# Sorted experts: rings of eight blocks, destinations read in place, the second bias staged with the weights, experts chosen by maxima, part 0 placed ahead of later projections

## The reference

```python
x = _layernorm(x + L1_attn(x, ...))
logits = flat_x @ W_router + b_router              # 2048 tokens, 8 experts
top_vals, top_idx = jax.lax.top_k(logits, 2)
w = softmax over the two chosen logits
for e in range(8):
    h = relu(flat_x @ W1[e] + b1[e])               # 128 -> 512
    y = h @ W2[e] + b2[e]                          # 512 -> 128
    final_output += y * w[:, e]                    # 0 for tokens that did not choose e
x = _layernorm(x + final_output)
```

## Time and profile before

| | us |
|---|---|
| median of 3 runs | 2021.28 (2018.37 to 2021.78) |
| profiled execution, its own time | 2016.37 |
| its span, first to last instruction | 2014.6 |

### The profile page before, as it was taken

The page is one execution under the profiler, slowest core; times in us unless marked ns, Lnnn a source line. Parts: engine busy times, 40 slices in busy tenths (PEclk is TensorE's granted clock), DMA queues, the critical chain, the costliest instruction groups (busy, mean ns, idle before and its releaser), DMA issues. The chain is left out here.

```text
span 2014.6 us, 42506 instructions
## 1 busy us (share of the span) xinstructions
PE 1725.4 (86%) x15741; PEld 1463.1 (73%) x15741; DVE 1403.6 (70%) x3312; ACT 999.9 (50%) x2616; POOL 605.6 (30%) x1005
## 2 busy tenths in 40 slices
PE   3599999899999999999993797999999999986583
PEld 2577778788778778787872564788888888876473
DVE  4688777787777887777873675666666666645456
ACT  2355555555555555555551324566565656533242
POOL 6255335554345553345450000000000000013431
PEclk9799999999999999999996798999999999996797
DMA  4122332123332323322331104940000000020112
GB/s 187 53 70 62 72 82 73 43 70 74 72 82 52 64 62 71 83 65 57 76 62 41 45 0 63 116 2 1 1 2 2 1 2 1 1 85 24 51 54 82
DMA packets 145232, 106.20 MB, mean 53 GB/s; under 512 B 32068, under 2 KB 134296, under 8 KB 144008
## 3 DMA queue, kind: packets, MB, share of 16 engines
q1 hardware_dynamic: 142760, 98.85, 23.3%
q0 software_dynamic: 2272, 4.67, 0.7%
HBM read 86.39 MB, written 17.10 MB: 51 GB/s over the span
## 5 line engine op out<-in xcount | busy, mean ns | idle before, releaser
L577 POOL TENSOR_TENSOR kfull<-kt,pair_rows 128x512 f32<-128x512 f32 x128 | 143.9, 1124 | 514.2 <-ACT kt L365 504.2
L345 PE MATMUL ps<-xT,taps 128*128 128x128 f32 x2176 | 295.0, 278 | 0.1
L345 PEld LDWEIGHTS ps<-xT,taps 128*128 128x128 f32 x2176 | 275.6, 197 | 8.0 <-issue 7.6
L830 ACT COPY wt<-ps 32x128 f32<-32x128 f32 x512 | 131.7, 257 | 259.4 <-PE ps L726 253.1
L1562 DVE TENSOR_REDUCE b_nmax<-ps 128x1 f32<-128x128 f32 (+7 forms) x256 | 180.4, 752 | 73.0 <-PE ps L1397 73.0
L873 DVE TENSOR_TENSOR prod<-ps,mt 128x128 f32<-128x128 f32 x512 | 147.1, 287 | 74.6 <-PE ps L737 59.3
L726 PE MATMUL ps<-ident,w 128*128 128x128 f32 x512 | 162.3, 317 | 34.2 <-ACT wt L830 19.8
L1539 POOL COPY b_spread<-b_inv 128x256 f32<-128x256 f32 x64 | 25.8, 403 | 512.9 <-DVE b_inv L1565 512.9
L876 DVE TENSOR_REDUCE w<-prod 128x32 f32<-128x128 f32 x512 | 146.5, 286 | 17.5
L726 PEld LDWEIGHTS ps<-ident,w 128*128 128x128 f32 x512 | 87.8, 171 | 84.8 <-DVE w L876 73.4
L1489 ACT ACTIVATE b_prob_long<-ps,b_nmax 128x1024 f32<-128x1024 f32 (+3 forms) x128 | 121.4, 953 | 55.7 <-DVE b_nmax L1562 55.7
(11 more groups left out here) (294 smaller groups left out, 3881.5 us busy)
## 6 DMA issues: line engine op xcount, KB each, us to landing
decay<-ends_dram SPq DMA_DIRECT2D x256, 128.0 KB, 5.8
gn<-near_dram SPq DMA_DIRECT2D x34, 384.0 KB, 6.8
rr<-rates_dram SPq DMA_DIRECT2D x34, 256.0 KB, 4.6
sq<-rstd_dram SPq DMA_DIRECT2D x17, 512.0 KB, 3.7
slots_dram<-zero SPq DMA_DIRECT2D x1, 8704.0 KB, 60.8
wtap<-in_taps SPq DMA_DIRECT2D x4, 1024.0 KB, 11.3
f_w<-in_f_w SPq DMA_DIRECT2D x2, 2048.0 KB
s_xb<-slots_dram SPq DMA_DIRECT2D x39, 64.5 KB, 1.8
```

The lines of the kernel that those rows point to most:

```text
L345: mm = pe.matmul(part, lhsT=taps[:, tap, t * P:(t + 1) * P], rhs=xT[:, :, columns(at_next) - LOOK + tap:columns(at_next) - LOOK + tap + TS ...
L577: nc.gpsimd.tensor_tensor(kfull[:, n % 4, :, :], kt[:, n % 2, :].unsqueeze(1).to_broadcast([P, G, P]), cst["pair_rows"][:, :].unsqueeze(2) ...
L830: nc.scalar.copy(wt[rows, b, :], ps[rows, 2, 0:P]).then_inc(wt_kept[b], 1)
```

## The change

- The rings of x rows and results have eight buffers (`AHEAD`). The wait for the scatter of block k-8 stands in `keep_y` and in SP's load, no longer in `stage`; `stage` waits for `y_kept` of block k-3 instead.
- Destinations are stored as integers in the rows' last column, and the scatter reads them there; the cast and `y_i` are gone. The fill of empty slots writes integers too.
- b1 and b2 lie beside w2 (`DOWN` = 644 columns for each expert), and one copy stages all. `keep_y` adds b2. The bias matmuls, the transposes of the weights and the four adds are gone.
- `choose` takes the maximum twice (`pick`) and works on 32 columns. The difference of the two scores is kept, one Exp over all tiles runs on ACT at block 2, and `share_out` at block 8 turns it into shares.
- `positions` adds the counts of earlier tiles up in PSUM by 8 matmuls instead of 2; `place_rows` is shorter.
- Order: part 0 is normalized, chosen and placed ahead of part 1's norm; projections of parts 1 and 3 are cut in halves, with `turn_x(0)`, `logit(0)` and `positions(1)` in between. ACT does part 2's squares ahead of `keep_x(1)`, and part 3's ahead of `keep_x(2)`.
- `HALVES` is 1, so all branches for more than one half are not taken; lines that serve them alone are left out here, as are declarations and the bodies that only vanish (`bias`, `weigh`, `exponent`, `keep_comb`, the old `choose` and the loops that called them), which stand in the kernel above.

```diff
-    nc.gpsimd.memset(blank[2][:, :], 0.0).then_inc(fill_made, 1)
-    pool.wait_ge(fill_made, 2)
-    nc.gpsimd.tensor_copy(blank[1][:, :], blank[0][:, :]).then_inc(fill_made, 1)
+    nc.gpsimd.memset(blank[1][:, :], 0.0).then_inc(fill_made, 1)
...
-SLOTS = NT * P
...
+SLOTS = NT * P // HALVES
+BLOCKS = TOP * NT // HALVES + NE - 1
+STRETCH = NE * SLOTS + NE * P
...
-        if k >= 4:
-            sp.wait_ge(S["x_turned"], k - 3)
-            sp.wait_ge(S["staged"], k - 3)
...
+    for k in range(K):
...
+        if k >= AHEAD:
+            sp.wait_ge(y_out[k % AHEAD], 16 * (k // AHEAD))
+        at = sp.value_load(table_i[0:1, 0, k:k + 1], min_val=0, max_val=HALVES * STRETCH - P)
+        sp.dma_start(xb[:, k % AHEAD, :], x_dram[bass.ds(at, P), :]).then_inc(xb_in[k % AHEAD], 16)
...
+    def send_result(k):
+        pool.wait_ge(S["y_kept"], k + 1)
+        nc.gpsimd.indirect_dma_start(
+            out=y_dram[:, :], out_offset=bass.IndirectOffsetOnAxis(
+                ap=xb[:, k % AHEAD, C:ROW].bitcast(U32), axis=0),
+            in_=yb[:, k % AHEAD, :], in_offset=None).then_inc(y_out[k % AHEAD], 16)
...
+    for t in range(GT):
+        ch.step(nc.gpsimd.tensor_copy(row[:, t, :, :, C:ROW].bitcast(I32), place[:, t, :, :, :]))
...
-        pe.wait_ge(S["made"], 1)
-        chosen = of(sel, s).rearrange("p t e -> p (t e)")
-        pe.matmul(small(s)[:, 32:64], lhsT=before[:, :], rhs=chosen, start=True, stop=True, skip_group_check=True)
-        pe.matmul(small(s)[:, 64:96], lhsT=ones[:, :], rhs=chosen, start=True, stop=True,
-                  skip_group_check=True).then_inc(S["pos_done"], 1)
...
+        if s == 0:
+            pe.wait_ge(S["made"], 1)
+        mine = of(sel, s).rearrange("p t e -> p (t e)")
+        pe.matmul(small(s)[:, 32:64], lhsT=before[:, :], rhs=mine, start=True, stop=False, skip_group_check=True)
+        for t in range(1, GT):
+            pe.matmul(small(s)[:, 32 + t * NE:64], lhsT=ones[:, :], rhs=mine[:, 0:(GT - t) * NE], start=False,
+                      stop=(t == GT - 1), skip_group_check=True)
         for t in range(GT):
...
+            mm = pe.matmul(small(s)[:, 64:64 + NE], lhsT=ones[:, :], rhs=mine[:, t * NE:(t + 1) * NE], start=(t == 0),
+                           stop=(t == GT - 1), skip_group_check=True)
+        mm.then_inc(S["pos_done"], 1)
...
-        if k < 2:
-            pe.wait_ge(S["bias_added"], 1)
-        else:
+        if k == 0:
+            pe.wait_ge(S["slotted"], PARTS - 1)
+            pe.wait_ge(S["in_done"], PARTS)
+        if k >= 2:
             pe.wait_ge(S["rect_a"], k - 1)
             pe.wait_ge(S["rect_v"], k - 1)
...
-        if k < 2:
-            pe.wait_ge(S["bias_added"], 1)
-        else:
+        if k >= 2:
             pe.wait_ge(S["y_kept"], k - 1)
+        if k == 1:
+            pe.wait_ge(S["slotted"], PARTS)
...
     project(0)
-    project(1)
+    project(1, range(0, 2))
     turn_x(0)
     logit(0)
+    project(1, range(2, GT))
+    positions(0)
     project(2)
-    positions(0)
     turn_x(1)
     logit(1)
-    project(3)
-    bias(0)
+    project(3, range(0, 2))
+    positions(1)
+    project(3, range(2, GT))
     turn_x(2)
     logit(2)
-    positions(1)
-    bias(1)
+    positions(2)
     turn_x(3)
     logit(3)
-    positions(2)
-    bias(2)
-    positions(3)
-    bias(3)
+    if HALVES == 1:
+        positions(3)
...
+    squares(0)
+    root(0)
+    keep_x(0)
+    squares(1)
+    root(1)
+    squares(2)
+    keep_x(1)
+    root(2)
+    squares(3)
+    keep_x(2)
+    root(3)
+    keep_x(3)
+    keep_block(0)
...
+        rectify(k)
+        if k == 2:
+            act.wait_ge(S["gaps"], PARTS)
+            nc.scalar.activation(share[:, 1, :], best[:, :, 1], ACT.Exp).then_inc(S["exp_done"], 1)
...
+    def pick(s, w):
+        level = of(best, s)[:, :, w]
+        mine = chosen[:, s, w, :, :]
+        ch.step(reduce(level, score[:, :, :], axis=AX.X, op=ALU.max))
+        ch.step(tt(hit[:, :, :], score[:, :, :], level.unsqueeze(2).to_broadcast(square), ALU.is_equal))
+        ch.step(tt(hit[:, :, :], hit[:, :, :], order[:, :].unsqueeze(1).to_broadcast(square), ALU.mult))
+        ch.step(reduce(where[:, :], hit[:, :, :], axis=AX.X, op=ALU.max))
+        ch.step(tt(mine, hit[:, :, :], where[:, :].unsqueeze(2).to_broadcast(square), ALU.is_equal))
     def choose(s):
         dve.wait_ge(S["logits"], s + 1)
...
         if s == 0:
             dve.wait_ge(S["made"], 1)
...
+        ch.step(tt(score[:, :, :], small(s)[:, 0:32].rearrange("p (t e) -> p t e", t=GT),
+                   br[:, :].unsqueeze(1).to_broadcast(square), ALU.add))
+        pick(s, 0)
+        ch.step(nc.vector.scalar_tensor_tensor(out=score[:, :, :], in0=chosen[:, s, 0, :, :], scalar=LOWEST,
+                                               in1=score[:, :, :], op0=ALU.mult, op1=ALU.add))
+        pick(s, 1)
+        tt(of(sel, s), chosen[:, s, 0, :, :], chosen[:, s, 1, :, :], ALU.add).then_inc(S["sel_done"], 1)
+        tt(of(best, s)[:, :, 1], of(best, s)[:, :, 1], of(best, s)[:, :, 0], ALU.subtract).then_inc(S["gaps"], 1)
+    def place_rows(s):
+        g, i = divmod(s, PG)
+        dve.wait_ge(S["pos_done"], s + 1)
+        ch.step(tt(slot[:, :, :], small(s)[:, 32:64].rearrange("p (t e) -> p t e", t=GT),
+                   seen[:, g, i, :].unsqueeze(1).to_broadcast(square), ALU.add))
+        ch.step(tt(seen[:, g, i + 1, :], small(s)[:, 64:64 + NE], seen[:, g, i, :], ALU.add))
+        by = [P, TOP, GT, NE]
+        ch.step(tt(picked[:, :, :, :], chosen[:, s, :, :, :], slot[:, :, :].unsqueeze(1).to_broadcast(by), ALU.mult))
+        ch.step(reduce(pair[:, :, :], picked[:, :, :, :], axis=AX.X, op=ALU.add))
+        ts(slot_i[:, s, :, :], pair[:, :, :], float(g * STRETCH), None, ALU.add).then_inc(S["slotted"], 1)
...
         if k >= 2:
-            dve.wait_ge(S["down_done"], k - 2)
             dve.wait_ge(S["up_done"], k - 1)
         if k >= 3:
+            dve.wait_ge(S["y_kept"], k - 2)
             dve.wait_ge(S["rect_a"], k - 2)
-        if k >= 4:
-            dve.wait_ge(y_out[k % 4], 16 * (k // 4))
         e = dve.value_load(table_i[0:1, 1, k:k + 1], min_val=0, max_val=NE - 1)
         nc.vector.tensor_copy(w1s[:, k % 2, :], w1[:, bass.ds(e * F1, F1)])
-        nc.vector.tensor_copy(w2s[:, k % 3, :, :], w2[:, bass.ds(e * J, J), :])
-        nc.vector.tensor_copy(b1s[:, k % 3, :], b1[:, bass.ds(e * J, J)])
-        dve.wait_ge(xb_in[k % 4], 16 * (k // 4 + 1))
-        nc.vector.tensor_copy(y_i[:, k % 4, :], xb[:, k % 4, C:ROW]).then_inc(S["staged"], 1)
+        nc.vector.tensor_copy(w2s[:, k % 3, :], w2[:, bass.ds(e * DOWN, DOWN)]).then_inc(S["staged"], 1)
...
     def keep_y(k):
         dve.wait_ge(S["down_done"], k + 1)
-        nc.vector.tensor_copy(yb[:, k % 4, :], ps[:, k % 2, 0:C]).then_inc(S["y_kept"], 1)
...
+        if k >= AHEAD:
+            dve.wait_ge(y_out[k % AHEAD], 16 * (k // AHEAD))
+        tt(yb[:, k % AHEAD, :], ps[:, k % 2, 0:C], w2s[:, k % 3, F1 + J:DOWN], ALU.add).then_inc(S["y_kept"], 1)
+    def share_out():
+        dve.wait_ge(S["exp_done"], 1)
+        ch.step(ts(share[:, 0, :], share[:, 1, :], 1.0, None, ALU.add))
+        ch.step(nc.vector.reciprocal(share[:, 0, :], share[:, 0, :]))
+        ch.step(tt(share[:, 1, :], share[:, 1, :], share[:, 0, :], ALU.mult))
...
+    add_projected(0)
+    centre(0, "centred")
+    variance(0, "squared", "summed")
+    scale(0, "rooted", "in_done")
+    dve.wait_ge(S["wr_in"], 16 * len(loads[0]))
+    choose(0)
+    place_rows(0)
+    add_projected(1)
+    centre(1, "centred")
+    variance(1, "squared", "summed")
+    scale(1, "rooted", "in_done")
+    for s in range(2, PARTS):
+        add_projected(s)
+        centre(s, "centred")
+        choose(s - 1)
+        variance(s, "squared", "summed")
+        place_rows(s - 1)
+        scale(s, "rooted", "in_done")
...
+        choose(3)
+        place_rows(3)
+        make_table(0)
+        stage(0)
...
+    for k in range(K):
+        g, kk = divmod(k, BLOCKS)
+        if k + 1 < K:
             stage(k + 1)
...
         rectify(k)
         if k >= 1:
             keep_y(k - 1)
...
+        if k == 8:
+            share_out()
...
+down = w2[:, :].rearrange("p (e f) -> p e f", e=NE)
+f1_pairs = [(w1[:, :].rearrange("c (e f) -> c e f", e=NE), d["f1_w1"]),
+        (down[:, :, 0:F1], d["f1_w2"].rearrange("p (e j) c -> p e (j c)", e=NE)),
+        (down[:, :, F1:F1 + J], d["f1_b1"].rearrange("p (e j) -> p e j", e=NE)),
+        (down[:, :, F1 + J:DOWN], d["f1_b2"].partition_broadcast(P))]
```

More of the change, by code:

```diff
@@ L1610, in sparse_experts @@
+        place = sb("place", [P, GT, TOP, NT // GT, 1], I32)
         total, mean, var, std = (sb(n, [P, NT]) for n in ("total", "mean", "var", "std"))
         sq = sb("sq", [P, NT, C])
[L1612 to L1621, removed]
+        score, hit, first, second = (sb(n, [P, GT, NE]) for n in ("score", "hit", "first", "second"))
+        best = sb("best", [P, NT, TOP])
+        where = sb("where", [P, GT])
```

(35 more changed lines are left out.)

388 lines of the change are left out of this document (172 added, 216 removed).

## The result

| | before | after |
|---|---|---|
| median in one measurement, us | 2019.82 (2017.10 to 2021.78) | 1999.47 (1996.44 to 2000.46) |
| profiled span, us | 2014.6 | 1994.7 |

The ratio of the times is 0.9898 (95% interval 0.9880 to 0.9915): 20.4 us faster, where 2003.5 us and 17.8 us less were predicted. The spans differ by 19.9 us. The stage starts at 1784.65 us, 1.3 us earlier than before and ahead of every step that I costed. Of the rest the routing (up to the last scatter's start) gave 12.1, from there to `up(0)` 1.7, from `up(0)` to the first result 0.2, the loop 4.5, the tail 0.1.

A forecast was written before the change was run, and what follows sets the result against it. Late destinations with 24 queued scatters were taken to bound routing, the ring of four the blocks. Terms -12.6, -2.3, -4.1 and +1.2 sum to -17.8 us, taking the 2021.3 us median to 2003.5; range 1988 to 2012.

The forecast's parts named there:

- What bounds the kernel now: Last stage: late part 1 destinations, then 24 queued scatters in routing; in the blocks, the ring of four awaiting scatter landings.
- Routing, -12.6: Routing: the new order brings the last scatter 16.6 us earlier, less 4.0 for clock: -12.6 us, between -7 and -19.
- The 4.0 charged for the clock: Routing: TensorE's idle gaps of 2.1, 3.0 and 3.0 us lower its clock; 4.0 us charged, bounds 0 and 9.
- B: Rival, block loop: TensorE paces at 1.95 to 2.05 us a block, about 1991 us in total; chance 0.27.
- Start of the blocks, -2.3: From the last routing scatter's landing to `up(0)`: 3.8 us instead of 6.1, with bias adds and ring casts gone.
- Period, 2.35: Block loop: VectorE paces at 2.35 us a block, with register load exposed and a scatter collision; loop -4.1 us.
- +1.2 for Exp and `share_out`: Block loop: `share_out` adds 0.7 us on VectorE and the Exp's table load 0.5 on ScalarE, +1.2 us together.
- Tail, fill: After the last result (30.8 us) nothing changes; the removed POOL cast beside attention is covered by TensorE: 0.
- C: Rival, block loop: each `w1s` copy waits a scatter out, period 2.55 us, 2010.5 us in total; chance 0.07.
- D: Rival, routing: TensorE at half clock through parts 1 to 3 of the projection, 14 us more, 2017.5 us; chance 0.05.
- E: Rival: no change, 2017.3 to 2025.3 us, as a block loop at 2.85 us eats the routing's gain; chance 0.03.
- F: Rival, block loop: `y_kept` wait and register load take 1.5 us, period 3.1, slower at 2029.5 us; chance 0.03.

The follow-up runs named there:

- the fourth buffer: The changed kernel with four places instead of three for the staged `w2s`, so `stage` waits for a result one block older: 1987.2 us, ratio 0.9834.
- the register: The changed kernel with the expert number of block k+1 loaded into a register behind block k's copies: 1981.7 us, ratio 0.9809.
- the last kernel: The changed kernel with row copies ahead of squares, two matmuls for positions, register load a block ahead, `up(0)` before `turn_block(1)`: 1971.9 us, ratio 0.9760.
- both routing edits: The changed kernel with row copies ahead of the next squares on ScalarE and positions by two matmuls: 1986.7 us, ratio 0.9834.
- the order of before: The changed kernel's functions with the earlier kernel's routing order on TensorE, ScalarE and VectorE: 2011.8 us, ratio 0.9974.

## Why the prediction was right, step by step

- **The sum**: the costed steps gave 18.6 us where 17.8 were forecast, with errors of both signs: the routing gave 0.5 and the start 0.4 less, the loop with its additions 1.6 more. That these nearly cancel is luck. The other 1.3 us of the spans' 19.9 is the chance in the stage's start. Of the 4.0 us between 2003.5 and 1999.5, 1.5 is the median of before (2021.3 in the rows, 2019.8 beside the change).
- **What bounds the kernel now**: right. The routing's gain came from the order, which has part 1's destinations ready earlier, and VectorE paces the blocks, as the runs with the fourth buffer and the register show. That the ring's wait paced the blocks before is read from the rows of before alone (29 of 35 stages start 3.1 to 3.2 us behind the scatter they wait for); no run isolates it.
- **Routing, -12.6**: measured -12.1. The order gives it, as worked. The first scatter of each part, by the time from the stage's start, came 2.2, 4.2, 4.3 and 4.2 us later than my steps without the clock (slots plus 0.3). The 4.0 charged for the clock is about the size of that: two half projections took 5.44 and 5.92 us, not 3.82, 3.7 in all, and part 1's logits 0.8 more than at full clock; other steps were a little shorter. That positions and logits would be at half clock in parts 2 and 3 was right too (1.88 and 3.6 us). ScalarE's new order I had noted in the steps but not priced by itself: 8.8 us more were to be had there. Two slips of adding: part 3's terms come to 1853.1 and not 1853.4, and B with the routing at its better bound to 1985 and not 1986.
- **Start of the blocks, -2.3**: measured -1.7 to `up(0)` from the last scatter's start; behind the landing 4.5 us pass and not 3.8 (6.1 before). Failed: "After the landing stay SP's issue, the load, one transpose, and the copy". `turn_block(1)` stands ahead of `up(0)` and waits for the second load (1872.27); `up(0)` starts 0.97 us after its own input's copy began. In the last kernel it started 0.83 us after the first transpose began and not 1.48, but as the rows came late there, the time shows nothing of it.
- **Period, 2.35**: measured 2.32. `w1s` at +1.09 (1.08 predicted), body 1.01 without the collision (1.00), collision 0.21 (0.25), each with a run behind it.
- **+1.2 for Exp and `share_out`**: 0.3. The table load and the Exp lay in ScalarE's slack, no period is longer there. `share_out` put one `w1s` copy 0.5 us later, and so past the scatter: that period is 0.30 longer. Of the 1.6 us by which the loop gained more than the sum, this is 0.9, and 0.03 us a period over 35 blocks is 1.1; against them stand two periods 0.13 longer each (the one behind `share_out`'s and one at block 21, both with `w1s` 0.35 later, cause not found) and a slightly longer end.
- **Tail, fill**: no change, 0.1.
- **Rivals.** B's period came only when the register load left the path or the wait had slack, so it was not the change's. C is excluded: it wants 2.55. The Trainium skill, SBUF — State Buffer, "SBUF: two separate sides", has the port pair of VectorE and GpSimd held for a whole instruction. The rows disagree in one direction: a copy that starts 0.26 into a scatter (1921.60) takes its usual 0.49. In the other they show a part of it: a scatter that starts 0.08 us behind a copy of 0.43 takes 1.18 and not 0.96, 0.22 more where waiting the copy out would be 0.35. D was not there: the projections lost about 4 us to the clock, as the forecast had charged, and not 18. E and F needed a period of 2.85 or 2.97.

## What to carry to other kernels

Price the order of every in-order queue as you price its instructions: two parts' copies, each behind the next part's squares, were 8.8 us here, 4.9 of waiting and 3.9 of TensorE's clock, which fell in the gaps. When a wait for a transfer is replaced by one for an engine's own last instruction, a register load behind it stands bare on the path (0.6 us of each block's path; without it the period fell by 0.42, 15 us in all, to TensorE's pace); load it a block ahead. A buffer that a transfer reads in place stays taken until that transfer lands, so check the ring's length against it: four buffers in place of eight cost some 75 us here.

## What the runs showed of the hardware

- A 512-column copy on VectorE that begins 0.51 to 0.73 us into one of GpSimd's scatters of 0.96 us is over 0.22 or 0.23 us after the scatter, so that it takes from 0.68 down to 0.45 us (1887.22 is one, 0.53 in). One that begins 0.12 to 0.50 in, or from 0.78 on, takes its usual 0.41 to 0.43. This holds in all kernels here; a copy of 644 columns is over 0.29 after it.
- In the kernel with both routing edits and in the last one the table's instructions, the same in all, took 10.8 and 13.8 us from the first one's start to the last one's, and not 4.5. Timeline of the last kernel:

```profile
1849.07 0.17 DVE L1988 TENSOR_TENSOR s_upto<-s_upto,s_blocks 128x8 f32<-128x8 f32 x1 [1.18 <-DVE s_upto L1987]
1849.78 0.23 DVE L1989 TENSOR_SCALAR s_jump<-s_blocks 128x8 f32<-128x8 f32 x1 [0.55 <-DVE s_upto L1988]
...
1851.17 0.48 DVE L1991 TENSOR_TENSOR s_passed<-s_upto,s_count 128x312 f32<-128x312 f32 x1 [1.15 <-DVE s_jump L1989]
```

Nearly all of this is idle time between instructions, mostly 0.4 to 1.2 us where the kernel after has 0.03 to 0.04. Both are kernels in which GpSimd sends 24 scatters back to back; but so does the order of before, with a table of 4.5 us. The cause is open. In the last kernel it costs 2.2 us: the table ends at 1857.65, after the last landing (1856.0), and the first load starts at 1859.16. With both routing edits alone it costs nothing by itself, as the table ends at 1854.51 and the last scatter lands at 1855.90; the 0.9 us there are idle time in SyncE's own list, between its register load and the first block's load, with the cause open too.
